# A decoder layer on one core: a new order of the opening, root on VectorE, and name columns spread over 15 slots

## The reference, cut to what matters

```python
x = x + attn(layernorm(x))       # per head h: q, k, v = silu(x W)
                                 # o = (q k^T * exp(-s_h (i - j)), i >= j) v
                                 # out = (sigmoid(x Wg) * norm_w * rmsnorm(o)) Wo
x = x + xattn(layernorm(x))      # softmax over ctx rows, masked
x = x + ffn(layernorm(x))        # fp8-rounded gate, up, down with reorder indices

def _reorder_quantize_x(x, idx):
    scale = jnp.max(jnp.abs(x)) / GLOBAL_DIV
    xr = (x / scale)[:, idx]
    scale_x = jnp.max(jnp.abs(xr), axis=1, keepdims=True) / FP8_MAX
    return _fp8(xr / scale_x), scale_x, scale
def _qlinear(qx, scale_x, scale, W, idx, out_idx=None):
    Wr = W[:, idx]
    w_scale = jnp.max(jnp.abs(Wr), axis=1, keepdims=True) / FP8_MAX
    qw = _fp8(Wr / w_scale)
    y = qx * scale_x @ (qw * w_scale).T * scale
    return y if out_idx is None else y[:, out_idx]
```

## Time and profile before

| what | us |
|---|---|
| median of 3 runs (2721.32 to 2723.69) | 2723.68 |
| the profiled execution | 2728.08 |
| its span | 2726.3 |
| PE busy (97% of the span) | 2657.1 |
| DVE busy (77%) | 2104.0 |
| ACT busy (41%) | 1119.0 |
| POOL busy (27%) | 729.9 |

### The profile page before, as it was taken

How to read it: one execution, slowest core, us unless ns; L and a number is a source line. 1 busy time by engine, 2 the same in 40 slices (tenths; PEclk the granted TensorE clock), 3 DMA queues, 4 the chain that set the end, 5 groups by cost and what they waited for, 6 DMA issues and landing times.

```text
span 2726.3 us, 40939 instructions
## 1 busy us (share of the span) xinstructions
PE 2657.1 (97%) x14711; PEld 2199.5 (81%) x14711; DVE 2104.0 (77%) x3806; ACT 1119.0 (41%) x1882; POOL 729.9 (27%) x952
## 2 busy tenths in 40 slices
PE   6999899999999999999999999999999999999996
PEld 5888788888888888888888888888876666666663
DVE  7788977887787787778788867866747777777777
ACT  4433333433343343334344323433325555555554
POOL 3111211211131121113112111211124444444444
PEclk9999999999999999999999999999999999999998
DMA  6553322342243225323343333423373344434420
GB/s 220 185 210 143 128 99 103 110 171 101 103 156 125 101 103 145 136 101 134 118 153 117 129 110 122 155 93 118 107 266 111 119 128 122 130 118 127 130 80 23
DMA packets 119015, 351.00 MB, mean 129 GB/s; under 512 B 15776, under 2 KB 18720, under 8 KB 110112
## 3 DMA queue, kind: packets, MB, share of 16 engines
q1 hardware_dynamic: 116480, 339.74, 36.2%
q0 software_dynamic: 2336, 8.65, 1.0%
HBM read 251.75 MB, written 96.61 MB: 128 GB/s over the span
## 4 chain that ended last, share of the span: by engine, by line
PE 93%; DVE 3%; issue 2%; DMA 1%; ACT 1%; POOL 0%; SPq 0%; POOLq 0%; DVEq 0%; ACTq 0%
PE bank L704 38%; PE bank L713 13%; PE bank L1359 13%; PE bank L828 9%; PE bank L788 8%; PE bank L1413 5%; PE bank L1436 3%; PE bank L1391 1%; PE bank L1382 1%; DMA attention_x_in<-in_x 1%; PE bank L1427 1%; PE bank L1371 0%; DVE attention_stats L885 0%; SPq L361 0%; PE bank L746 0%
## 5 line engine op out<-in xcount | busy, mean ns | idle before, releaser
L704 PE MATMUL bank<-attention_xT,attention_w_hi 128*128 128x512 f32 x3072 | 956.7, 393 | 3.0 <-DVE attention_xT L894 2.6
L704 PEld LDWEIGHTS bank<-attention_xT,attention_w_hi 128*128 128x128 f32 x3072 | 568.8, 189 | 115.1 <-issue 3.5
L704 PE MATMUL bank<-attention_xT,attention_w_lo 128*128 128x512 f32 x1536 | 599.7, 390 | 0.0
L531 POOL TENSOR_TENSOR attention_sq_sum<-attention_sq_sum,attention_sq 128x512 f32<-128x512 f32 x128 | 206.3, 1612 | 1228.9 <-ACT attention_sq L676 1228.9
L713 PE MATMUL bank<-attention_w_hi,attention_xT 128*128 128x256 f32 x2048 | 383.0, 287 | 3.7 <-DVE attention_sig_v L851 3.7
L704 PEld LDWEIGHTS bank<-attention_xT,attention_w_lo 128*128 128x128 f32 x1536 | 288.9, 188 | 62.1
L713 PEld LDWEIGHTS bank<-attention_w_hi,attention_xT 128*128 128x128 f32 x2048 | 320.6, 193 | 3.9 <-DVE attention_sig_v L851 3.9
L713 PE MATMUL bank<-attention_w_lo,attention_xT 128*128 128x256 f32 x1024 | 290.9, 284 | 0.0
L984 DVE TENSOR_TENSOR attention_sf<-bank,attention_dcy 128x512 f32<-128x512 f32 (+1 forms) x256 | 147.8, 619 | 172.5 <-PE bank L788 172.4
L1359 PE MATMUL bank<-finish_w_out_hi,finish_og 128*128 128x512 f32 x824 | 280.1, 401 | 0.2
L996 DVE TENSOR_TENSOR attention_sl<-attention_sf,attention_sh 128x384 fp32r<-128x384 f32 (+1 forms) x384 | 242.7, 687 | 0.0
(11 more groups left out here) (201 smaller groups left out, 5056.9 us busy)
## 6 DMA issues: line engine op xcount, KB each, us to landing
attention_xT<-normed_turned SPq DMA_DIRECT2D x62, 2048.0 KB, 8.5
gated_heads<-attention_og_out SPq DMA_DIRECT2D x64, 1024.0 KB, 7.7
finish_og<-gated_heads SPq DMA_DIRECT2D x103, 512.0 KB, 3.8
finish_og_last<-gated_heads SPq DMA_DIRECT2D x25, 512.0 KB, 3.8
normed_turned<-attention_shared SPq DMA_DIRECT2D x24, 512.0 KB, 6.8
attention_shared<-in_w_head SPq DMA_DIRECT2D x16, 512.0 KB, 7.3
finish_x<-in_x SPq DMA_DIRECT2D x32, 256.0 KB, 4.2
out<-finish_x SPq DMA_DIRECT2D x32, 256.0 KB, 4.3
```

Source lines behind the costliest of these rows:

```text
L531: g.tensor_tensor(sq_sum[:, col_b], sq_sum[:, col_b], sq[:, :], ALU.add).then_inc(s_acc, 1)
L704: mm = pe.matmul(dst[:, :], part[a][w][:, k, col:col + P], xT[i][:, b, k, :], start=(k == 0 and s == 0), stop=(k == KD - 1 and s == 2))
```

## The change

**Loads.** x of batch 0 comes in four transfers with a semaphore each; the slope is loaded from ACT's queue; V's weights come ahead of batch 1's x.

**First normalising.** For batches 0 and 1, root and mean are computed on DVE (`root_of`), no longer on POOL. Batch 0 is normalised half on ACT (tiles 0, 1), half on DVE (tiles 2, 3).

**First projection.** The weights of QK0 are split in four blocks (`s_w0h`, `s_w0l`), and Q's matmuls start block by block. The fourth block of turned x lies in `G_BANK`, so that `Q_BANK` is free. K follows, then values(0), then the turning of batch 1, and values(1) into `O_BANK`. In slot 0 Q and K of the next head stand before the scores.

**Products of ones.** `keep_warm`: 60 matmuls of 128 columns at PE's start and 24 before Q; in `finish`, three of 512 columns in each of four places of the steps 29 to 34.

**Statistics of batch 2** move on DVE from before slot 0 into slot 0, behind `sl`.

**Names.** One column a slot, in slots 11 to 25; PE sums them in slots 26 and 27, and the row tasks begin at FIRST = 28 instead of 18.

**Small.** `sq_sum` is copied in each batch's first slot instead of cleared and added; three semaphores (`s_mag`, `s_xa`, `s_ta`) are dropped; the last tile's sum is added on DVE.

```diff
-    NAMED = 2 * B
+    COLUMNS = max(PREPARED) + 1
+    NAMED = COLUMNS + 1 + KD + KF
     FIRST = NAMED + 2
     STEP = 3
...
+    SUMMED = {COLUMNS + 1 + k: k for k in range(KD + KF)}
...
     def x_banks(m):
-        return (*S_BANK, G_BANK if m == 1 else Q_BANK)
+        return (*S_BANK, G_BANK if m < 2 else Q_BANK)
...
+    def v_bank(half):
+        return O_BANK if half == 1 else V_BANK
...
     # sync
-        sp.dma_start(slope_b[:, :], slope.to_broadcast([P, NH])).then_inc(s_slope, 16)
-        load_x(0)
+        for t in range(KT):
+            sp.dma_start(x_buf[0][:, t, :], x_tiles[t]).then_inc(s_x0[t], 16)
         load_raw(QK0_W, 0)
+        load_raw(V_W, 0)
         load_x(1)
-        load_raw(V_W, 0)
         load_raw(QK1_W, 0)
+        load_raw(G_W, 0)
         load_x(2)
-        load_raw(G_W, 0)
...
     # gpsimd
-        g.memset(sq_sum[:, :], 0.0).then_inc(s_zero, 1)
-        norm(0)
-        norm(1)
         weights_lo(V_W, 0)
-        norm(2)
         weights_lo(QK1_W, 0)
         weights_lo(G_W, 0)
+        norm(2)
...
     # scalar
-        weights_hi(QK0_W, 0)
-        normed(0)
+        nc.scalar.activation(warm[:, :], dist[:, 0:1], ACT.Sigmoid)
+        act.wait_ge(s_nb, 1)
+        for t in range(KT // 2):
+            nc.scalar.activation(x_buf[0][:, t, :], x_buf[0][:, t, :], ACT.Identity, bias=nb[:, 0, t:t + 1],
+                                 scale=rs[:, 0, t:t + 1]).then_inc(s_n0, 1)
+        act.wait_ge(s_raw[QK0_W], 16)
+        for k in range(KD):
+            nc.scalar.copy(part[0][QK0_W][:, k, :], raw_part(QK0_W, k)).then_inc(s_w0h, 1)
+            x_hi(0, k)
         weights_hi(V_W, 0)
...
     # tensor
+        def keep_warm(times):
+            for _ in range(times):
+                pe.matmul(V_BANK[:, 0:P], ones16[:, :], ones16[:, :], start=True, stop=True, skip_group_check=True)
...
+        pe.wait_ge(s_pool, 1)
+        keep_warm(60)
+        pe.wait_ge(s_pool, 4)
+        for t in (0, 2, 1, 3):
...
+        keep_warm(24)
+        for k in range(KD):
+            pe.wait_ge(s_w0h, k + 1)
+            pe.wait_ge(s_w0l, k + 1)
+            pe.wait_ge(s_xl, k + 1)
...
+        wait_part(V_W, 0)
+        values(0, 0)
         for k in range(KD):
             turn_x(1, k)
-        wait_part(V_W, 0)
-        values(0, 0)
-        pe.wait_ge(s_vm, 1)
-        values(1, 0)
+        values(1, 0, v_bank(1))
...
+            if n == 0:
+                next_head(n, p, i, j, wrap)
...
-            if not last:
...
+            if not last and n:
+                next_head(n, p, i, j, wrap)
...
     # vector
+        root_of(0)
+        v_.wait_ge(s_nb, 1)
+        for t in range(KT // 2, KT):
+            shifted(0, t).then_inc(s_n0v, 1)
         for k in range(KD):
+            v_.wait_ge(s_w0h, k + 1)
+            v_.tensor_tensor(part[1][QK0_W][:, k, :], raw_part(QK0_W, k), part[0][QK0_W][:, k, :].bitcast(F32),
+                             ALU.subtract).then_inc(s_w0l, 1)
             x_lo(0, k)
+        all_stats_of(1)
+        root_of(1)
+        queries(0)
...
-        stats_of(2)
...
+            if n == 0:
+                all_stats_of(PREPARED[0])
...
-            for k in SUMMED.get(n, ()):
-                add_name(k)
+            if n in SUMMED:
+                add_name(SUMMED[n])
...
     # finish, tensor
+        def keep_warm():
+            pe.wait_ge(s_x1, T)
+            for _ in range(3):
+                pe.matmul(Y_BANK[:, :], early.ones16[:, :], upT[:, 0:4, 0, :], start=True, stop=True,
+                          skip_group_check=True)
...
             if tile(n + 3):
                 project(n + 3, 0)
+            elif n + 3 >= T:
+                keep_warm()
...
     # finish, vector (and the counterpart skipped on gpsimd)
+            if m == T - 1:
+                v.wait_ge(s_yo, T)
+                v.tensor_tensor(xr[m % SLOTS][:, :], yo[:, :], xr[m % SLOTS][:, :], ALU.add).then_inc(s_x3, 1)
```

223 lines of the change are left out of this document (125 added, 98 removed).

## The result

Over 20 runs each, the changed kernel takes 2729.39 us and the one before 2723.82: ratio 1.0021, interval 1.0015 to 1.0027. That is 5.6 us slower (4.1 to 7.4); forecast were 2729, 0.2% slower. The two profiled executions do not show the difference: their spans are 2725.7 after and 2726.3 before. "Slot 1" is the start of its projection (Q and K of the next slot, then the gate), "127" the start of the gate of the last slot.

A forecast was written before the change was run, and what follows sets the result against it. PE was taken to work almost throughout, so edits pay only at its idle or low-clock stretches. Opening +8.0, names -2.6, tail +0.4 gave +5.8 on the median 2723.68: 2729 us, range 2718 to 2735.

The forecast's parts named there:

- the 8.0: Opening: us lost at the start of slot 1's scores, 69.7 against 61.63.
- the 2.6: Names in all: us won, from 7.3 won in slots 14 and 15 and 4.7 lost in later refreshes.
- Opening up to slot 0: Start to slot 0's scores: VectorE sets the pace, slot 0 opens at 38.9, its scores end at 46.9.
- The rival in which small products are not held: Opening: the lock doesn't hold small products; opening +5.5, sum +3.3, 2727.0 us; chance 0.24.
- What the opening gives back: Slot 0: batch 2's later statistics idle PE 8.8 us, slow outputs of 3.7 follow; slot 1 starts at 69.7.
- my mark: Start of slot 1's scores, 61.63 in the profile before; by what it moves, the rest moves.
- Names: Slots 14 and 15: idleness and low clock fall from 8.8 to 1.5 us, 7.3 won.
- Phase: Refreshes 30 to 94: other row work stands ahead of them, costs go from 11.7 to 16.1, 4.7 us lost.
- the rival in which it costs nothing: Later refreshes: something else sets the waits at 30, 62 and 78; sum +1.1, 2724.8 us; chance 0.10.
- Tail: From step 29: the ones and the last sum together -1.0 to +1.7 us, middle taken, +0.4.
- The rival in which all is faster by the clock alone: Whole kernel: new order and ones leave PE at 2.4 GHz; sum -6.9, 2716.8 us; chance 0.12.
- Slower by more: Rival: gate's weights_lo meets values ahead of slot 0, tail's ones at low clock; +9.6, 2733.3 us; chance 0.18.

The follow-up runs named there:

- e_lock: The changed kernel with one wait on GpSimd, splitting QK1's weights only once the first queries are through; 2729.91 us, 1.0017 of the kernel before.
- the second profile of before: The kernel before, unedited, timed and profiled once more; 2725.86 us, ratio 1.0000, profile span 2722.7 us.
- e_names: The kernel before with only the changed names (one column a slot in slots 11 to 25, row tasks from 28); 2717.50 us, ratio 0.9975.
- e_open: The changed kernel with names and row tasks as before, leaving the new opening, the ones and the last sum; 2734.26 us, 1.0033 of the kernel before.
- e_phase: The changed kernel with the row tasks beginning at slot 30 instead of 28; 2723.94 us, 0.9998 of the kernel before.
- e_tail: The changed kernel without the 72 products of ones in the last six steps; 2728.34 us, 1.0017 of the kernel before.
- e_ones: The changed kernel without the 84 products of ones at its start; 2728.96 us, 1.0016 of the kernel before.
- the second of after: The changed kernel, unedited, timed and profiled once more; 2730.23 us, 1.0020 of the kernel before, profile span 2726.8 us.
- e_stats: The changed kernel with the statistics of batch 2 moved back ahead of slot 0 on VectorE; 2722.66 us, 0.9994 of the kernel before.

## Why the prediction was right, and which of its steps were not

The number was right and the sign too, but two terms of the sum were off in opposite directions: by all but the first profile of before the opening costs 1 to 3 us more than the 8.0, and the names win up to 5 more than the 2.6. That they nearly cancel, and that the sum meets the 5.6 of the medians within 0.2, is luck; the profiles add up to 3 to 4.

**Opening up to slot 0: right, with a slip.** Forecast were first transposes near 12.4 (12.19), the end of x's low part of batch 0 near 19.5 (19.3), the collision of QK1's split with the root at 24.9 for 2.45 (24.79, 2.2 lost). The rival in which small products are not held fell: the 2.34 at 24.84 is such a product, `e_lock` shows its cause, and the rule of the Trainium skill (SBUF — State Buffer, Who interferes with whom) held in that size plays no part. That no row showed an instruction of that size held was not so: GpSimd's step at 11.44 in the trace of before (2.04 for 1.02, beside a VectorE instruction that began 0.09 earlier) is one, and it spoke against this rival beforehand. VectorE was ready at 38.1 instead of 38.9, and PE began Q and K at 37.8 without waiting for it, so the scores ended at 45.2 instead of 46.9. Of that 1.7, 0.6 is a slip of addition: 38.9 + 5.5 + 1.85 is 46.3.

**What the opening gives back: the idleness right, two terms missed.** 8.8 us were forecast behind the gate and 8.74 came; slow outputs came behind it too, but 2.9 long and not 3.7. Slot 1's scores started at 67.0 (forecast 69.7; 1.7 of the difference is that of the scores of slot 0, most of the rest is those outputs). But my mark was the start of the scores, and VectorE's queue behind it (`og`, statistics of batch 3, last low part) held the projection for 1.7 more: 7.2 lost against the first profile. The other step that failed is the mark's own value for before. I measured against 61.63 of one execution; in the second profile of before the scores of slot 1 start at 58.1, in `e_names` at 59.4. I had noted that the profiled execution lay 4.4 above the median and then carried the difference over as if it lay evenly. Against the second profile the opening costs 10.7, against `e_names` 9.4, and `e_open` has 9.0 in the medians, for the 8.0 (and 0.4 for the tail) of the sum.

**Names: right in mechanism, mis-sized.** In slots 14 and 15 all 10.0 us went, the 11.3 of the table less the 1.3 of PE's sums over names, which moved to slots 26 and 27. I had kept 1.5 back for what might stay in them: with 0.9 instead of 5.25 in slot 13 nothing stayed. 7.3 was the term, 10.0 the measurement; beside the 1.5, 1.2 was missed in slot 15, which was 2.2 longer than a plain slot before, not 1.05.

**Phase: right, somewhat smaller.** Waits of 3.23, 3.24 and 1.9 came in slots 30, 78, 46 and 94 and none in 62, exactly by kind. The cost was 2.6 (3.9 from slot 18 to 127 less the 1.3 moved there) instead of 4.7, as the low clock behind two of them was short (2.10 for the 12 outputs in slots 46 and 94, where I had a mean of 2.10 and 3.56), and as the refresh at 94, priced at 0.5, had cost 1.1 before (slot 95, 16.0 for 14.9). The price of scaling was read from the wrong slot: the 3.56 is that of slot 78, and the outputs of slot 62 took 2.72 in before; as its values were slow as well (3.83 for 2.9), the slot was 5.0 longer than a plain one, and the 4.9 is right all the same. `e_phase` shows that the start of the row tasks is worth 5.5 us, part of it because slot 29 then holds none, so the rival in which it costs nothing fell. In the profiles the names won 7.4 in all, and 6.8 in `e_names`, for the 2.6 of the sum; the step from `e_open` to the changed kernel leaves 3.3.

**Tail: right.** +1.4 for the ones, -0.6 for the last sum, and the low clock at down(30) not mended by them; the middle of the range was +0.4. In the stretch as a whole nothing shows (738.8 and 739.1 for 738.7 and 739.0), because down(30) took 0.8 less in both profiles of after; as its length goes from 4.0 to 4.9 with ones and without, that is not put down to them. The rival in which all is faster by the clock alone fell: neither in the tail nor at the start do the ones hold the upper level (`e_tail`, `e_ones`), and the outputs behind the idleness of slot 0 took 2.9, not the 1.9 by which it was to be decided. Its terms were added wrongly besides: 2.1 - 7.3 + 1.3 - 1.0 is -4.9 and not -6.9, or 2718.8, which lies within the 0.2%. The advice of the Trainium skill (TensorE: Matmul & The Clock Gate, Why this matters for your kernels) against gaps, set beside the sum in the prediction, would have given 1.0 won; the runs show 1.4 lost.

**Slower by more: not in the two profiles.** That GpSimd's split of the gate meets the values ahead of slot 0 did not come in either profile of after. It came in `e_phase`, with the same program up to there, and put slot 1 1.7 later. So it depends on the execution, and some of the runs behind the median of after may hold it; how many is not shown.

Against the second profile of before the terms make 10.7 - 10.0 + 2.6 - 0.2 = +3.1 (spans 2725.7 and 2722.7), and +4.1 with the second of after. The medians are 5.6 apart; the last 1.5 to 2.5 us of it no pair of profiles shows, and they stay open. They have the size of the differences between executions of one kernel: 2726.45 to 2734.34 among the other 19 runs of after.

## What to carry to other kernels

When a start-up is rebuilt to begin earlier, follow the slowest engine's queue to the first steady slot: here VectorE's 17 us of work behind the first scores, and one group of statistics put behind them, decided, not what was won at the start. Work that is due at a fixed rhythm should be laid around the periodic heavy slots by hand: the holes in the three-slot rhythm were worth 11.6 us (1642.8 for 1654.4 from slot 18 to 127), twice what the whole change moved. And before a profile's mark is used as the reference of a sum, its total is to be set against the median: 4 us of difference have a place, and it may be the very stretch that changes.

## What the runs showed of the hardware that I had not expected

- A step on 128 x 4 elements on VectorE is held for nearly the whole of a GpSimd instruction of 2.38 us (2.34 instead of 0.16), and by its timing so is one on GpSimd beside a VectorE instruction of 1.22 us (2.04 instead of 1.02). A shift with one SBUF tensor and columns as scalars is held as well (3.93 for four instead of 1.91), and so is a cast of 128 x 512 (1.95 instead of 0.43, `e_stats`).
- 60 products of ones that end 5.8 us ahead of the first transposes did not leave them at the upper level: the 16 took 3.35, for 3.65 without ones and 1.91 at the upper level.
- The same idleness ahead of the outputs is followed by a short or a long stretch at 1.2 GHz, from one execution to the next: behind 1.9 us in slot 46 the 12 outputs took 2.10 in `after` and 3.45 in `e_tail`, and kernels whose program is the same there take 1654.1 to 1657.3 us from slot 18 to 127.
